# Two chained LoRA feed-forward layers on one core: x, x1, xT, T differences and down products in another order

## The reference

```python
gate = lora_add(x @ W_gate.T, x, A_gate, B_gate)      # adapters by itok_B_2_6, scaled by 0.5
up   = lora_add(x @ W_up.T, x, A_up, B_up)
act  = silu(gate) * up                                # 1376 features
down = lora_add(act @ W_down.T, act, A_down, B_down)
x1   = x + down @ sign(weight).T + bias0
cond = (x1 @ B[ids].T) @ A[ids].T                     # adapters by itok_B_4_50
out  = x1 + ffn(cond)                                 # dense W, bias, eight weighted adapters
```

## Time and profile before

| | |
|---|---|
| runs | 883.05, 893.37 and 891.04 us, median 891.04 |
| the profiled execution | 893.9 us |
| its span, first to last instruction | 891.8 us |
| mean granted TensorE clock | 0.994 |
| PE (TensorE) busy | 857.4 us, 96% |
| DVE (VectorE) busy | 644.5 us, 72% |
| ACT (ScalarE) busy | 289.9 us, 33% |
| POOL (GpSimd) busy | 99.5 us, 11% |
| moved by DMA | 227.31 MB, mean 255 GB/s |

### The profile page before, as it was taken

How to read it: one execution, slowest core, us unless ns; L and a number is a source line. 1 busy time by engine, 2 the same in 40 slices (tenths; PEclk the granted TensorE clock), 3 DMA queues, 4 the chain that set the end, 5 groups by cost and what they waited for, 6 DMA issues and landing times.

```text
span 891.8 us, 22271 instructions
## 1 busy us (share of the span) xinstructions
PE 857.4 (96%) x7384; PEld 699.8 (78%) x7384; DVE 644.5 (72%) x1354; ACT 289.9 (33%) x535; POOL 99.5 (11%) x130
## 2 busy tenths in 40 slices
PE   8998899998999999999999999999999999999897
PEld 5886688886788788888888888878788788878785
DVE  5695676866768586877868686877868586877764
ACT  4861432322333232333333232322333232323310
POOL 0256000100000000000000000000000000000001
PEclk9999999999999999999999999999999999999999
DMA  9977877877877797888879787888779697888753
GB/s 337 415 257 251 311 222 227 253 243 251 263 249 214 219 298 246 273 278 270 272 240 260 233 258 244 286 264 271 234 255 254 218 293 246 279 266 272 232 142 102
DMA packets 171356, 227.31 MB, mean 255 GB/s; under 512 B 59200, under 2 KB 128832, under 8 KB 163648
## 3 DMA queue, kind: packets, MB, share of 16 engines
q1 hardware_dynamic: 112800, 114.47, 43.6%
q10 hardware_dynamic: 56096, 103.37, 33.7%
q0 software_dynamic: 2432, 9.11, 2.7%
HBM read 178.69 MB, written 16.97 MB: 219 GB/s over the span
## 4 chain that ended last, share of the span: by engine, by line
PE 64%; DMA 13%; SPq 9%; DVE 7%; issue 3%; ACTq 1%; ACT 1%; POOL 0%; DVEq 0%
PE gu_ps L1238 33%; PE y_ps L1359 19%; DMA x_landed<-x_in 6%; SPq L370 3%; DMA x_in<-in_x 2%; PE out_ps L1381 2%; PE gu_ps L1468 2%; PE out_ps L1432 2%; SPq L396 2%; DMA landed<-act_all 1%; SPq L462 1%; SPq L457 1%; DMA xT_raw<-in_xT 1%; PE out_ps L1368 1%; DVE act_all L923 1%
## 5 line engine op out<-in xcount | busy, mean ns | idle before, releaser
L1359 PE MATMUL y_ps<-down_sb,actT_sb 128*128 128x512 f32 x1023 | 247.9, 395 | 0.0
L1359 PEld LDWEIGHTS y_ps<-down_sb,actT_sb 128*128 128x128 f32 x1023 | 189.7, 188 | 59.4 <-issue 21.4
L571 POOL TENSOR_TENSOR b_two<-b_raw,const_sb 128x128 f32<-128x128 f32 x62 | 23.8, 404 | 684.8 <-DMA b_raw<-in_b1tab 684.8
L640 ACT CAST actT_sb<-landed 128x512 fp32r<-128x512 f32 (+1 forms) x96 | 51.8, 582 | 148.1 <-issue 114.8
L1238 PE MATMUL gu_ps<-wg_sb,xT_sb 128*128 128x432 f32 x384 | 84.1, 369 | 2.8 <-DVE act_all L923 2.8
L1238 PE MATMUL gu_ps<-wu_sb,xT_sb 128*128 128x432 f32 x384 | 81.7, 361 | 0.0
L1238 PEld LDWEIGHTS gu_ps<-wg_sb,xT_sb 128*128 128x128 f32 x384 | 72.9, 193 | 8.1 <-DVE xT_sb L905 3.7
L1238 PEld LDWEIGHTS gu_ps<-wu_sb,xT_sb 128*128 128x128 f32 x384 | 71.0, 188 | 4.0
L1238 PE MATMUL gu_ps<-slot,s_sb 128*128 128x512 f32 x270 | 69.0, 391 | 0.0
L927 DVE STREAM_TRANSPOSE act_all<-act_all 128x512 f32<-128x512 f32 (+1 forms) x96 | 64.1, 667 | 3.3
L640 ACT COPY ad_two<-a_raw 128x352 f32<-128x352 f32 x64 | 28.0, 484 | 118.2 <-PE out_ps L1381 114.5
(11 more groups left out here) (188 smaller groups left out, 1295.0 us busy)
## 6 DMA issues: line engine op xcount, KB each, us to landing
slot<-t_table ACTq DMA_DIRECT2D x59, 1024.0 KB, 8.0
vslot_raw<-vt_table ACTq DMA_DIRECT2D x60, 432.0 KB, 4.5
a_raw<-in_atab SPq DMA_DIRECT2D x128, 152.0 KB, 8.0
rows_sb<-in_btab SPq DMA_DIRECT2D x128, 118.0 KB, 3.6
landed<-act_all SPq DMA_DIRECT2D x192, 64.0 KB, 3.1
xT_raw<-in_xT SPq DMA_DIRECT2D x32, 256.0 KB, 3.8
x_in<-in_x SPq DMA_DIRECT2D x31, 256.0 KB, 9.9
out_x<-out_sb SPq DMA_DIRECT2D x31, 256.0 KB, 6.1
```

The lines of the kernel that those rows point to most:

```text
L571: nc.gpsimd.tensor_tensor(b1_two[:, n].rearrange("p k e r -> p e k r"), rows, ones, ALU.mult).then_inc(L["b1_moved"], 1)
L640: return nc.scalar.copy(o, i)
L1359: last = nc.tensor.matmul(to[:], actT_sb[:, ACTT_SLOT[c] + n, a, :], down_sb[:, blk, b, :], start=begin and (c, n) == (0, 0) and (a, b) == ...
```

## The change

- SyncE loads x of group g at the end of step g, behind the B rows, when x1 of `prev` has left x_in (a new wait on x1T_in), not x of `prev` ahead of the B1 rows. Only x of group 0 is loaded as before.
- xT is loaded by ScalarE's queue, right behind the copy of lhs, ahead of its loads of T and vt.
- SyncE sends the x1 pieces ahead of the C rows in odd steps.
- In even steps ScalarE sends its x1 pieces ahead of the cast of s4; in odd steps it casts s1 and s2 behind the Silus.
- VectorE splits s1 and s2 behind the gating, and vslot 1 and 2 behind add_y and turn_x1.
- The differences of T and vt are made by VectorE: those of T ahead of its first low_t in step 0, those of vt behind the gating of step 0. GpSimd only stores; the stores of vt1 and vt3 stand behind T2's, those of vt2 and vt4 behind T4's, with a signal each.
- In the last step TensorE makes the first nine down products behind the row products, not before them; the first of the rows then opens y_ps.

```diff
@@ SyncE
                 sp.wait_ge(L["ad_moved"], PAIRS * (g + 1))
-                if after_next is not None:
-                    load_xT(after_next, parity)
...
                         sp.wait_ge(S["last_out"], 2 * 32)
-                    load_x(prev)
+                        load_x(prev)
                     load_b1(prev, post)
...
-                    if prev is not None:
+                    if prev is not None and parity == 1:
+                        send_x1(sp, prev, range(2, 4))
+                        load_c(sp, post)
+                    elif prev is not None:
                         load_c(sp, post)
                         send_x1(sp, prev, range(2, 4))
                     load_b(next_cond)
+                    if prev is not None:
+                        sp.wait_ge(L["x1T_in"], SENT * (prev + 1))
+                        load_x(g)
@@ GpSimd
-            difference(t1_raw, t3_raw, t1_raw)
...
+            def side_store(n, signal):
+                pool.wait_ge(S["vt_raw"], 4)
+                pool.dma_start(vt_table[n - 1], vt_raw[n][:].rearrange("p k w -> p (k w)")).then_inc(signal, 16)
+
             t_store(1, S["first_out"])
...
             t_store(2, S["first_out"])
+            side_store(1, S["vt13_out"])
+            side_store(3, S["vt13_out"])
             t_store(3, S["last_out"])
             t_store(4, S["last_out"])
+            side_store(2, S["vt24_out"])
+            side_store(4, S["vt24_out"])
@@ ScalarE
                     copy_q1(j)
+                    send_x1(act, pp, range(0, 2))
                     high_s(4, j)
                     load_side_t(3)
-                    send_x1(act, pp, range(0, 2))
                 if isinstance(g, int) and g == 1:
-                    act.wait_ge(S["vt_out"], 4 * 16)
+                    act.wait_ge(S["vt13_out"], 2 * 16)
...
                 copy_lhs(g)
+                if after_next is not None:
+                    load_xT(act, after_next, parity)
...
+                    if not seven(j):
+                        act.wait_ge(S["vt24_out"], 2 * 16)
                     load_side_t(1)
...
+                for c in range(NC):
+                    silu(g, c)
                 if parity == 1 and nxt is not None:
                     high_s(1, j + 1)
                     high_s(2, j + 1)
-                for c in range(NC):
-                    silu(g, c)
@@ VectorE
+            def differences(raw, signal):
+                def difference(o, a, b):
+                    nc.vector.tensor_tensor(raw[o][:], raw[a][:], raw[b][:], ALU.subtract).then_inc(signal, 1)
+
+                difference(1, 3, 1)
...
                 if first(g):
-                    dve.wait_ge(S["t_raw"], t_count(2))
+                    dve.wait_ge(S["raw1_in"], 2 * 16)
+                    dve.wait_ge(S["raw2_in"], 2 * 16)
+                    differences(t_raw, S["t_raw"])
                     low_t(1)
...
-                if parity == 1 and nxt is not None:
-                    low_s(1, j + 1)
-                    low_s(2, j + 1)
...
                 if parity == 1 and nxt is not None:
-                    low_side_t(1, j + 1)
-                    low_side_t(2, j + 1)
+                    low_s(1, j + 1)
+                    low_s(2, j + 1)
                 if first(g):
+                    dve.wait_ge(S["vraw_in"], 4 * 16)
+                    differences(vt_raw, S["vt_raw"])
                     low_t(3)
                     low_t(4)
...
                     add_y(prev)
                     turn_x1(prev)
+                if parity == 1 and nxt is not None:
+                    low_side_t(1, j + 1)
+                    low_side_t(2, j + 1)
@@ TensorE
                     after(pe, L["x1_done"], prev)
-                    down(prev, 0, begin=True).then_inc(L["y_mm"], 1)
+                    if not last(g):
+                        down(prev, 0, begin=True).then_inc(L["y_mm"], 1)
                 lora_ready(g, j, parity, prev, pp)
-                first_rows(prev, pp)
+                first_rows(prev, pp, last(g))
                 second_rows()
                 if prev is not None:
-                    for c in range(1, NC):
+                    for c in range(0 if last(g) else 1, NC):
                         down(prev, c).then_inc(L["y_mm"], 1)
```

67 lines of the change are left out of this document (24 added, 43 removed).

## The result

| | before | after |
|---|---|---|
| median of the runs | 891.52 us (4 runs, 883.05 to 893.37) | 864.43 us (4 runs, 863.64 to 866.17) |
| the profiled execution | 893.9 us, span 891.8 | 864.41 us, span 862.5 |
| mean granted TensorE clock | 0.994 | 1.0 |
| PE busy | 857.4 us, 96% | 851.8 us, 99% |

The changed kernel takes 0.9709 of the time before, 95% interval 0.9652 to 0.9767: 26 us less, by the medians 27.1 us, and by the two profiled executions 29.3 us of span. I had said 873 us with a range of 861 to 886, so the time lies in the range and 8.6 us under the number. The sign held, and the waits that were to go are gone; one term measured 0 in place of +6.0 us, others were too small, and the experiments show that xT's move, which I had entered as nothing, is what keeps the new place of x from costing more than it brings.

What follows compares the result with a forecast made beforehand. PE bounds the loop, busy 647.56 of 666.00 us. Terms -14.3 - 2.0 + 6.0 - 8.1 + 0 = -18.4 us on 893.9 give 875.5, less 2.5 for luck 873 us; range 862 to 882, with two rivals 861 to 886.

Steps and rivals of the forecast that it cites:

- Waits for x1, -14.3: Loop, even steps: PE's waits for x1's copy before the small products all go, 14.3 us less.
- New vslot wait, +6.0: Loop: vslot splits behind x1 make PE wait 0.4 us in each of 15 pairs, bounds 0 to 24 us.
- Gating wait, -2.0: Loop: of PE's 3.31 us wait for VectorE's gating before 214.31 us, 2 us go with xT's earlier issue.
- xT, "I take the issue as equal ... I add nothing": Loop: xT's move to ScalarE leaves its 3.8 us median landing unchanged, bounds -0.5 and +1 us.
- xT lands late: slower: Rival, loop: xT landing 3 us later in 15 pairs gives 912 us; no gain from 5.4 us landing; chance 0.06.
- Start, -8.1: Start: VectorE's differences shorten idle and slow-clock time, less a new T1 wait; net -8.1 us, bounds 0 and -10.3.
- Last step, 0: Last step: nine down products moved behind the row products change nothing, bounds -0.6 and +0.6 us.
- The 2.5 us taken off for luck: Whole kernel: 2.5 us subtracted because the profiled execution's two loop waits over 3 us were partly bad luck.

Runs made afterwards that it cites:

- before_x_sends: Kernel before with x loaded behind the B rows and both engines' x1 sends moved ahead, xT left on SyncE: 909.98 us (1.0223).
- before_start: Kernel before with the start's part alone, differences on VectorE and the new order of GpSimd's stores: 886.18 us (0.9939).
- bias_first: Changed kernel, but in its loop GpSimd adds the bias to x1 before moving the B1 rows: 865.73 us (0.9718).

## Why the prediction was right, and where its sizes were wrong

The two spans, step by step (PE's first product of step 4 and of step 30 as marks): up to step 4 159.50 against 151.63 us, from there to step 30 660.18 against 642.78, and to the end 72.12 against 68.09. That is 7.9, 17.4 and 4.0 us, together 29.3, where the sum had 18.4 for the profiled execution.

*Waits for x1, -14.3: right in size, half right in its reason.* All twelve are gone. But of the reason given, "the x1 chain is led by VectorE's order and then by the order in two issuing queues", the second half is enough. The vslot and s moves do nothing for these waits: 864.37 us without the former, 871.68 us on the kernel before without either. Nor does an earlier turn: in before_x_sends it ends at E+5.5, as before, and no wait is left, while with it at E+1.9 and ScalarE's send behind the cast of s4 13.9 us are back. And where the turn itself comes from I had misread as well: with the splits moved and x where it was PE waits 33 us for the vslots, since x, asked for behind 2 MB of slots, lands as late as the splits end, and I had read only the 0.36 us by which it outlasted them. x's new place takes away that wait, which the move of the splits would have made.

*New vslot wait, +6.0: the step that failed.* It measured 0. It came from "that is 2.3 us earlier", which put the end of the turn at E+3.1, and "GpSimd adds its bias to x1 the moment that x1 is turned". The turn ends at E+1.9, since the sums start 1.9 us earlier against E (1 us in the median over the pairs), and the add comes at E+4.8 to E+7.6 in the loop, behind the B1 rows' landing. In the loop of the kernel before the turn ends at E+4.6 or later, when GpSimd is done or nearly done with its B1 rows, and the add follows it within 0.3 us in 14 of 15 pairs, as in the earlier trace rows; with the earlier turn it is the B1 rows that set the add's time. The contention is real, 1.1 us, but even when it is brought about PE has room for it.

*Gating wait, -2.0: -3.3, and 0.9 us of smaller waits with it.* I had left 1.3 us of it out as uncertain. It isn't chance: before_start, which has xT as before, shows it at the same step with 3.09 us, and no run that leaves xT at its new place and ahead of the vslots has it.

*xT, "I take the issue as equal ... I add nothing": wrong in weight.* Its landing went from 3.8 to 3.3 us in the median, inside my bounds. But without this edit the new place of x costs 19 us on the kernel before (909.98 against 891.01) and 37 us on the changed one (901.17 against 864.43). The rival "xT lands late: slower", with 5.4 us of landing as the point at which it is no gain, described those kernels well: 5.8 and 5.2 us, and both slower (the second already a little under that point). It had 0.06 because I compared the queues and not what stands ahead of xT in them. Behind the sum stood the Trainium skill's "DMA: Bandwidth & Descriptors", section "Issuing engines are not separate DMA queues", by which, as I had read it, xT's median stays; the trace agrees that the engine is not what matters (5.0 us behind the vslots on ScalarE), and shows in 3.3 us that the place in the order is.

*Start, -8.1: -7.9.* The splits take 1.05 us where GpSimd's differences had stretched them to 2.66. PE goes on at 73.48 (said: 73.5), small products at 83.86 (84), the T1 slot late by 1.65 us (1.7). ScalarE stands 6.25 us for the T2 store in place of 17.80, and vt24_out holds its loads until 95.69 (said: 96 or 97):

```profile
80.36 2.00 ACT L623 CAST t_high_lo<-t_raw 128x1024 fp32r<-128x1024 f32 x2 [6.25 <-DMA t_table<-slot]
...
95.69 0.84 ACTq L656 DMA_DIRECT2D vslot_raw<-vt_table  x2
```

The Trainium skill's "SBUF — State Buffer", section "SBUF: two separate sides", has VectorE with two SBUF inputs and GpSimd exclude each other for a whole instruction; the 2.02 us of the add and 3.09 us of the splits in bias_first agree with it.

*Last step, 0: about 0.* The tail shrank by 4.0 us: 3.0 are the last x1 wait, and the 1.0 left isn't the moved products', since with their old place it was 0.7 us shorter still.

*Left out: the clock behind waits.* From step 4 to step 30 the kernel before loses 18.4 us against 641.8 us of PE's work, but its waits are 15.5 us. The other 2.9 are a slower clock. Windows of the kernel before, behind its waits of 2.10 us (at 280.52) and 1.96 us (at 632.88):

```profile
280.52:281.50 0.98, 0.98 (x61) 0.98 (x65) 0.00 (x0) 0.00 (x0) 0.00 (x0) 0.64 1.04 159
281.50:291.50 10.00, 10.00 (x100) 8.45 (x99) 6.19 (x19) 3.52 (x6) 0.00 (x0) 0.86 0.64 204
...
632.90:643.00 10.10, 10.10 (x158) 8.12 (x159) 6.70 (x20) 4.05 (x7) 0.00 (x0) 1.00 0.73 221
```

After the first PE has 0.64 and 0.86 of its clock, after the second all of it. I had counted this in the start and not in the loop. So the terms as measured: -14.3 - 3.3 - 0.9 - 2.9 in the loop and its last wait, -7.9 in the start, -1.0 in the tail, +1.0 for a new wait for B rows (at 194.69 us), which makes -29.3.

*The 2.5 us taken off for luck* are within what was found: over the three later sets of runs the medians of the kernel before are 893.51, 891.01 and 890.56 us, 0.4 to 3.3 below the profiled 893.9. The changed kernel varies by 2.5 us where the kernel before varies by 10 to 19: with the waits went their spread.

## What to carry to other kernels

When a wait ends with a copy that an engine issues late, look first at what stands ahead of that issue in the engine's own program: two sends moved ahead of a cast and of other rows took these 14.3 us away, with the data ready no earlier. When a transfer itself is slow, look at what every queue had issued ahead of it, not at its own queue or its own size alone: here 256 KB take 2.8 or 9.9 us by whether they are asked for before or behind 2 MB of slots, and moving one such load ahead of the large loads is worth 38 us in a kernel whose step starts depend on it. A wait of 0.36 us on the critical engine says nothing of how late its transfer is when other work stands in front of it; take the landing time, not the rest that the engine waited. Test the parts of a change in pairs as well, and the cheapest part alone: x's new place without xT's is a loss of 19 us, the splits' new place without x's one of 52 us against the whole change, and the two sends alone, which may be all that the x1 waits needed, I left untested.

## What was not expected of the hardware

- What was asked for earlier on either queue delays a load: x, issued 1.7 to 3.4 us behind ScalarE's slots, lands after 9.9 us in the median; issued ahead of them, after 2.8 us. (SyncE's own A rows, four of 152 KB, stand ahead of it as well in the first case; the two weren't separated for x.) xT behind 864 KB of vslots on the same queue takes 5.0 us, ahead of them 3.3.
- PE's waits of 1 to 3 us in nearly every pair cost more than themselves: 31.0 us of waits from step 4 to step 30 come with 12.9 us of slower work (clock 0.98 to 0.99), 15.5 us with 2.9. A single wait of the same length may cost nothing, as the one at 632.88 us did.
- Once PE waits at the begin of a step, it goes on doing so: with xT behind the vslots 13 of 15 even steps wait 0.2 to 2.6 us, though each wait gives VectorE that much more time. The trace shows why a later PE doesn't give xT its lead back: xT is issued behind the copy of lhs, which follows PE, and so 9.0 to 9.2 us ahead of the time at which PE is ready for the even step, in all 14 pairs of the loop. From the sums to PE's start it takes 4.05 us, so some 5.0 us are left from issue to sums; it took 5.2 to 7.6 us, and PE waited for what was over.
